# A mixer step between expert tiles: one of four late steps cut into pieces that follow expert tiles, tile loops written out as straight code

## What is computed

```python
xn = _layernorm(x)
# mixer, 256 inner channels, per sequence
x_proj, z = split(xn @ W_in.T)
x_conv = silu(causal_conv(x_proj, conv_w, 4 taps) + conv_b)
Bm, Cm, dt_in = split(x_conv @ W_x.T)
dt = softplus(dt_in @ W_dt.T + b_dt)
alpha = sigmoid(0.1 * dt)
gated = (1 - alpha) * sigmoid(mean(Bm)) * x_conv
h = scan(h = clip(alpha, 0.01, 0.99) * h + gated)      # along the sequence
y = (h * sigmoid(mean(Cm)) + D * x_conv) * silu(z)
mixer = y @ W_out.T
# experts, 8 with 256 hidden, top 2 of 8
h = silu(xt @ w1[e]) * (xt @ w3[e]);  y[e] = h @ w2[e]
moe = sum over the two chosen experts of probs * y[e]
out = x + mixer + moe
```

## Time and profile before

| | us |
|---|---|
| median of 3 runs | 474.4 (473.97 to 475.49) |
| span of the profiled execution | 553.9 |
| stage one, to the first `up` | 0 to 247.5 |
| stage two, to the end of `down(34)` | 247.5 to 483.0 |
| tail | 483.0 to 553.9 |

### The profile page before, as it was taken

The page is one execution under the profiler, slowest core; times in us unless marked ns, Lnnn a source line. Parts: engine busy times, 40 slices in busy tenths (PEclk is TensorE's granted clock), DMA queues, the critical chain, the costliest instruction groups (busy, mean ns, idle before and its releaser), DMA issues.

```text
span 553.9 us, 8718 instructions
## 1 busy us (share of the span) xinstructions
PE 459.8 (83%) x2440; PEld 324.4 (59%) x2440; DVE 394.6 (71%) x836; ACT 288.3 (52%) x406; POOL 312.4 (56%) x344
## 2 busy tenths in 40 slices
PE   0987646999999999879979869696987798979876
PEld 0884222445544455448867658585876688745455
DVE  5997551989999999878856675454635465549987
ACT  3772126878888888785533333232423232466880
POOL 4657763767767675711666656565665655663300
PEclk9999777899999999999989999797989898899999
DMA  9921114112121212235556544453543453209992
GB/s 249 283 84 52 54 64 163 50 36 83 49 77 44 82 44 72 78 98 152 164 172 179 168 134 143 120 147 122 156 135 113 126 162 107 71 2 189 243 210 80
DMA packets 48076, 65.91 MB, mean 119 GB/s; under 512 B 8424, under 2 KB 30223, under 8 KB 48048
## 3 DMA queue, kind: packets, MB, share of 16 engines
q1 hardware_dynamic: 36240, 39.56, 25.5%
q0 software_dynamic: 10656, 24.47, 16.1%
q10 hardware_dynamic: 1152, 1.57, 0.9%
HBM read 42.09 MB, written 33.83 MB: 137 GB/s over the span
## 4 chain that ended last, share of the span: by engine, by line
PE 31%; DVE 22%; another core or an unknown queue 18%; issue 16%; ACT 8%; SPq 2%; DMA 1%; DVEq 1%; ACTq 0%
PE PC L746 5%; PE PB L731 4%; PE PD L899 4%; DVE hbuf L1404 3%; PE PA L759 2%; DVE hbuf L1415 2%; DVE gbuf L1289 2%; PE PA L865 2%; PE PA L861 1%; DVE gbuf L1386 1%; DVE xnT L1690 1%; PE PA L862 1%; DVE y L1424 1%; DVE al L1389 1%
## 5 line engine op out<-in xcount | busy, mean ns | idle before, releaser
L614 POOL DMA_INDIRECT moe_out<-xnT,dst_u x142 | 143.1, 1008 | 114.7 <-DVE xnT L1690 51.2
L600 POOL DMA_INDIRECT moe_in<-xn,slot_u x128 | 137.7, 1076 | 65.6 <-issue 41.1
L1202 ACT ACTIVATE xn<-PA 128x1024 f32<-128x1024 f32 (+1 forms) x36 | 36.5, 1015 | 95.1 <-PE PA L865 52.0
L1629 DVE TENSOR_TENSOR xn<-xn,PB 128x1024 f32<-128x1024 f32 (+1 forms) x36 | 43.3, 1204 | 43.1 <-remote 19.0
L899 PE MATMUL PD<-xnT,xn 128*128 128x128 f32 x536 | 68.1, 281 | 6.1 <-DVE xnT L1690 5.7
L899 PEld LDWEIGHTS PD<-xnT,xn 128*128 128x128 f32 x536 | 64.2, 196 | 8.5 <-issue 4.9
L746 PE MATMUL PC<-xc,Wc 128*128 128x512 f32 x128 | 59.9, 612 | 2.8 <-ACT xc L1099 2.8
L759 PE MATMUL PA<-xnT,Wtap 128*128 (+4 forms) x128 | 59.1, 604 | 0.4 <-issue 0.4
L1690 DVE TENSOR_TENSOR xnT<-PD,slot_p 128x512 f32<-128x512 f32 (+1 forms) x36 | 24.5, 681 | 39.6 <-remote 35.1
L861 PE MATMUL PA<-xhi,whi 128*128 128x512 f32 x62 | 29.4, 474 | 26.6 <-ACT xhi L1196 16.7
L1196 ACT ACTIVATE xhi<-PD 128x512 fp32r<-128x512 f32 (+1 forms) x36 | 21.2, 589 | 49.7 <-remote 32.6
(11 more groups left out here) (244 smaller groups left out, 963.2 us busy)
## 6 DMA issues: line engine op xcount, KB each, us to landing
xnT<-moe_w SPq DMA_DIRECT2D x36, 256.0 KB
xn<-moe_in SPq DMA_DIRECT2D x31, 266.0 KB
out_dram<-moe_out POOLq DMA_DIRECT2D x12, 512.0 KB, 11.8
xnT<-moe_w SPq DMA_DIRECT2D x36, 128.0 KB
out_dram<-xacc SPq DMA_DIRECT2D x7, 512.0 KB, 10.0
moe_out<-xnT,dst_u POOLq DMA_INDIRECT x142
moe_in<-zrow SPq DMA_DIRECT2D x8, 266.0 KB
moe_w<-in_L_ffn_w_dram SPq DMA_DIRECT2D x2, 1024.0 KB
```

Of the source, the lines that this page charges most:

```text
L600: gp.indirect_dma_start(xs_dram, bass.IndirectOffsetOnAxis(ap=slot_u[:, k, j:j + 1], axis=0), xn_row[:, j, :], None).then_inc(s_scat, 16)
L614: gp.indirect_dma_start(yt_dram, bass.IndirectOffsetOnAxis(ap=dst_u[:, t, j:j + 1], axis=0), yo[t % OUTS][:, j, :], None, bounds_check=PAI ...
L1202: act.activation(halves(sil, t), halves(PA[:, :], t), ACT.Silu).then_inc(s_sil, 1)
L1629: ve.tensor_tensor(halves(hid[b], t), halves(sil, t), halves(PB[:, :], t), ALU.mult).then_inc(s_hid, 1)
```

## The change

With `INNER_STEPS = 1` all of step 12 runs in stage two, cut into twelve pieces. Piece n follows the tile in `INNER_AT` on every engine (tiles 1, 3, 6, 8, 11, 14, 17, 19, 21, 24, 27 and 30). The first five pieces of step 13 (`STEPS_B = 13`) follow tiles 31 to 35. So that PA, PB and PD stay with the experts, all of it goes through PC: ScalarE copies the gates out of PC to `held_g` (`hold_among`), and `gates`, `out`, `project`, `convolved` and `gated` get twins that write PC, a few matmuls each.

On TensorE the pieces are `spread`, `gates`, `out` and the two halves of `project` (pieces 1 to 5), two halves of `convolved` (8, 9) and `gated` (10). On ScalarE piece 6 is a table load, Exp, Ln and a table load back. On VectorE the pieces are the chain in eight parts, `turn`, `add_out`, `softplus` and three taps. The tail then starts at step 13 behind its `project`. The loops over tiles on TensorE, ScalarE and VectorE become straight code; the one on SyncE stays, with one 512 KB store (`store_base`, before ahead of its loop) now behind it. SyncE starts the first weight loads one mixer step earlier (it waits for 11, not 12).

```diff
+INNER_STEPS = 1
+STEPS_B = STEPS_A + INNER_STEPS
+CYCLE = 30 // INNER_STEPS
+INNER_AT = (1, 3, 6, 8, 11, 14, 17, 19, 21, 24, 27, 30)
@@ sync @@
-            sp.wait_ge(s_xp, 12)
-            sp.wait_ge(s_z, 12)
+            sp.wait_ge(s_xp, 11)
+            sp.wait_ge(s_z, 11)
...
-            store_base(STORED - 2)
             with sp.Fori(0, (FULL - 4) // 2) as i:
...
+            store_base(STORED - 2)
@@ tensor @@
+            def project_among(g, c_):
+                slot = g % SLOT3
+                if c_ == 1:
+                    pe.wait_ge(s_lt, g + 1)
+                else:
+                    pe.wait_ge(s_add, g)
+                for k in range(HALVES):
+                    last = pe.matmul(PC[:, c_ * GROUP:(c_ + 1) * GROUP], Wc[:, k, c_ * P:(c_ + 1) * P],
+                                     xc[:, slot, k, :], start=(k == 0), stop=(k == 1))
+                if c_ == 0:
+                    last.then_inc(s_u, 1)
...
+            def mixer_piece(g, at):
+                if at == 1:
+                    spread(g)
+                elif at == 2:
+                    gates_among(g)
+                elif at == 3:
+                    out(g, g % SLOT3, True)
+                elif at == 4:
+                    project_among(g, 1)
+                elif at == 5:
+                    project_among(g, 0)
+                elif at == 8 and g < STEPS_B:
+                    convolved_among(g, 0)
+                elif at == 9 and g < STEPS_B:
+                    convolved_among(g, 1)
+                elif at == 10 and g < STEPS_B:
+                    gated_among(g)
...
-            with pe.Fori(0, (FULL - 4) // 2) as i:
...
-            for t in range(2 + (FULL - 4) // 2 * 2, MOE_TILES):
+            for t in range(2, MOE_TILES):
...
                 down(t - 1, (t - 1) // 2, (t - 1) % 2, False)
-            project(STEPS_A, STEPS_A % SLOT3, True)
+                for piece in pieces(t):
+                    mixer_piece(*piece)
...
-            gates(STEPS_A, STEPS_A % SLOT3, True)
-            for g in range(STEPS_A, GROUPS - 1):
+            for g in range(STEPS_B, GROUPS - 1):
@@ scalar @@
+            def mixer_piece(g, at):
+                if at == 1:
+                    hold_among(g)
+                    decay_th(g)
+                elif at == 2:
+                    decay_al(g)
+                elif at == 4:
+                    row_tanh(g)
+                elif at == 5:
+                    abs_among(g)
+                elif at == 6 and g < STEPS_B:
+                    act.preload_act_table_set("natural_log_exp_and_others")
+                    logs_among(g)
+                    act.preload_act_table_set("silu_and_others")
...
-            with act.Fori(0, turns) as i:
...
+                for piece in pieces(t):
+                    mixer_piece(*piece)
...
-            for g in range(STEPS_A, GROUPS):
+            for g in range(STEPS_B, GROUPS):
@@ vector @@
+                if at == 3:
+                    chain_among(g, 0)
+                    turn(g)
+                elif at == 4:
+                    add_out(g)
+                    chain_among(g, 1)
...
+                elif at == 7:
+                    softplus(g)
...
+                elif at == 9:
+                    for j in range(1, TAPS):
+                        tap(g, j)
...
-            turn(STEPS_A)
-            softplus(STEPS_A)
-            for g in range(STEPS_A, GROUPS - 1):
+            g = STEPS_B
+            chain_among(g, 3)
+            chain_among(g, 4)
+            softplus(g)
+            for n in (5, 6, 7):
+                chain_among(g, n)
+            for g in range(STEPS_B, GROUPS - 1):
```

More of the change, by code:

```diff
@@ L360, in is_mixed, with among_tiles, holds, pieces @@
             return isinstance(t, int) and FULL <= t < HALF
+        def among_tiles(g):
+            return isinstance(g, int) and STEPS_A <= g <= STEPS_B
         def gate_rows(g):
-            return PC if isinstance(g, int) and g == STEPS_A else PD
+            return PC if among_tiles(g) else PD
+        def holds(g):
+            return g - STEPS_A + 2
         def gated_y(c):
-            if not isinstance(c, int) or c < STEPS_A:
+            if not isinstance(c, int) or c <= STEPS_B:
                 return y2
-            return (held_g, y2, y3)[(c - STEPS_A) % 3]
+            return (y2, held_g, y3)[(c - STEPS_B) % 3]
+        def pieces(t):
+            found = [(STEPS_A + n, at + 1) for n in range(INNER_STEPS) for at in range(len(INNER_AT))
+                     if n * CYCLE + INNER_AT[at] == t]
+            last = t - INNER_STEPS * CYCLE
+            return found + [(STEPS_B, last)] if last >= 1 else found
         @block.sync
@@ L832, in _, with gates_among @@
             pe.sem_inc(s_out, 1)
-            mixer(pe, mix, 0, STEPS_A)
+            mixer(pe, mix, 0, STEPS_A - 1)
+            mixer(pe, mix, STEPS_A - 1, STEPS_A)
+            def gates_among(g):
+                slot = g % SLOT3
+                pe.wait_ge(s_xc, g + 1)
+                pe.wait_ge(s_hold, holds(g))
+                for k in range(HALVES):
+                    for j in range(STRIPS):
+                        last = pe.matmul(PC[j * STRIP:(j + 1) * STRIP, GROUP:GROUP + P], WgS[:, k, :],
+                                         xc[:, slot, k, j * P:(j + 1) * P], start=(k == 0), stop=(k == 1))
+                last.then_inc(s_g, 1)
@@ new lines, in convolved_among @@
+            def convolved_among(g, part):
+                both = PC[:, 0:GROUP].rearrange("p (s l) -> p s l", s=SPG)
+                src = source(g).rearrange("p (s l) -> p s l", s=SPG)
+                if part == 0:
+                    pe.wait_ge(s_dt, g + 1)
+                    pe.matmul(PC[:, GROUP:2 * GROUP], WinT[:, P:2 * P], source(g), start=True, stop=True).then_inc(s_xr, 1)
+                for j in range(2 * part, 2 * part + 2):
+                    last = pe.matmul(both[:, :, j:SEQ], Wtap[:, TAPS - 1 - j, :], src[:, :, 0:SEQ - j],
+                                     start=(j == 0), stop=(j == TAPS - 1))
+                if part == 1:
+                    last.then_inc(s_xp, 1)
@@ L954, in _ @@
             g = GROUPS - 1
-            pe.wait_ge(s_add, g - 1)
-            gated(g - 1)
+            if g > STEPS_B:
+                pe.wait_ge(s_add, g - 1)
+                gated(g - 1)
+            else:
+                pe.wait_ge(s_yc, MOE_TILES)
             spread(g + 1)
-            out(g, g % SLOT3, True)
+            if g > STEPS_B:
+                out(g, g % SLOT3, True)
             pe.wait_ge(s_add, g)
@@ L1212, in tile_step, with hold_among, abs_among @@
                     round_x(t + 1, 1 - b)
+            def hold_among(g):
+                act.wait_ge(s_gb, g)
+                act.wait_ge(s_ch, (g - 2) * CHAIN + C_USED)
+                act.activation(held_g[:, :, :], PC[:, :].rearrange("p (n l) -> p n l", n=2), ACT.Copy).then_inc(s_hold, 1)
+            def abs_among(g):
+                act.wait_ge(s_u, g + 1)
+                act.wait_ge(s_th, g)
+                for c_ in range(HALVES):
+                    last = act.activation(ebuf[:, c_, :], PC[:, c_ * GROUP:(c_ + 1) * GROUP], ACT.Abs,
+                                          bias=bdt[:, c_:c_ + 1])
+                last.then_inc(s_abs, 1)
@@ L1231, in _ @@
             round_x(2, 0)
+            for piece in pieces(1):
+                mixer_piece(*piece)
             round_w(3, 1, 1, False)
```

173 lines of the change are left out of this document (97 added, 76 removed).

## The result

The changed kernel takes 483.44 us (median of 4 runs, 483.01 to 483.90), the kernel before 474.37 (4 runs, 473.97 to 475.49). The ratio is 1.0203, with a 95% interval of 1.0181 to 1.0225: 9 us, or 2%, slower. The forecast was 480.5, slower.

The account below looks back on a forecast made before the run. It took TensorE, with almost no idle time, to bound stage two and a ring of waits the tail: 474.4 + 17.3 (stage two) - 11.0 (tail) = 480.7, rounded to 480.5 us; range 467.5 to 488, its own case 477 to 485.

Parts of the forecast that it names:

- Stage two of a timed run, 179 us: Stage two before: 235.5 us in the trace less 56 us of waits on an unknown releaser, 5.1 us a tile.
- The step on which the forecast rested: TensorE in stage two of a timed run: close to nothing left, 0.1 us a tile, 5 us in all.
- Stage two +17.3: Stage two: 17.3 us of moved TensorE work, less 2 hidden, plus 2 of new waits, gives +17.3 us.
- the 2 forecast: Stage two, new waits: 2 us, bounds 0 and 6, from ScalarE's piece 6 at tile 14 making later work late.
- the 2 us taken off as hidden: Stage two: moved TensorE work hidden in idle time and short waits for `xlo`, 2 us, bounds 0 and 21.
- Tail by compute −12.6: Tail, compute engines: `down(34)` to the taps for step 14 shrinks from 24.5 to 11.9 us, 12.6 us shorter.
- The DMA side: Tail: DMA sums before end 13 us ahead of the program; after, about equal to compute; 1.6 us off, leaving −11.0.
- The stores: End of the tail: the last stores come while the sums still run, 3 to 4 us of stores behind the sums.
- The loops: Tile loops: removal costed at nothing, since the branch is already hidden under the matmuls.
- The table load: ScalarE's piece 6 at tile 14: 1.28 us per table load as in the trace, without the skill's drain of about 1.38.
- 560.2 if the holes stay: Whole kernel against its profiled time, with the unknown-releaser waits unchanged: 553.9 + 17.3 - 11.0 = 560.2 us.
- TensorE has room after all: Rival, stage two: 14 of 17.3 us hide in TensorE's idle time, giving 469 us; chance 0.20.

Follow-up runs that it names:

- straight: Kernel before with its tile loops on TensorE, ScalarE and VectorE written out and no piece moved; 473.78 us against 473.83, ratio 0.9995.
- room: Kernel before with written-out tile loops plus one unused fp32 matmul behind each of tiles 13 to 26; 479.63 us, ratio 1.0110.
- after: The changed kernel itself, as profiled on a quiet chip (span 481.4 us); timed 483.44 us against 474.37 for the kernel before, ratio 1.0203.
- straight_nosums: Kernel before with written-out tile loops, without 12 of 14 accumulating DMAs and GpSimd's end waits for the sums; 467.96 us, ratio to before 0.9863.
- after_nosums_warm: Changed kernel without 12 of 14 accumulating DMAs, with 25 unused matmuls in two TensorE waits of the tail; 548.28 us, ratio 0.9768, stalling chip.

## Why the prediction was right, and where its steps were not

**Stage two of a timed run, 179 us: right, by luck in part.** Straight shows 179.8. The prediction took 56 us out, in proportion to a chain share of 29.9%, and left a part of the holes in. On a quiet chip there are none at all, and 21 of the 55.7 us that go are no holes, but matmuls that take 178.5 us instead of 199.6. The step on which the forecast rested, that TensorE has no room, holds on quiet chips; room shows it, with 12.1 us more in stage two for 14 matmuls costed at 11.9.

**Stage two +17.3: too small by 3.1 us.** It is +20.4. TensorE's busy time grew by 196.6 - 178.5 = 18.1, against the 17.3 summed up from the earlier trace rows, and its gaps from 1.3 to 3.7, 2.4 against the 2 forecast. The term that failed is the 2 us taken off as hidden. There was next to nothing to hide in, 1.3 us of idle time in the whole stage. Of the new gaps 1.1 us belong to piece 6, the term for them, and 1.5 are the waits of tile 3, behind the copy `hold_among`, which the prediction had as hidden. It had the copy's length (2.4 us with `decay_th`) and not its wait for VectorE.

**Tail by compute −12.6: too large by 1.9, of which 0.4 came back later.** Behind `down(34)` the taps for step 14 start after 22.5 us in straight and 11.8 in after: −10.7. The part of after (11.9) was right. That of before was read as 27.2 less one hole of 2.66, and 2 us of the rest were still holes. From the taps to the last add it is 43.3 and 42.9 us. The half clock of `project(14)`, which was not foreseen, costs 1.1 us in its round, and the half clock that straight has in the window from 452 makes up for it.

**The DMA side: the step that was wrong.** It said that before ends 13 us behind its DMA traffic, and that the change makes the two about equal. In straight the DMA side ends the span, 8.8 us behind the last add, and leaving the sums out gains 5.8. Two terms were wrong.

The first is the row of scatters. The step took the last scatter at 10.9 us behind `down(34)` from a trace in which TensorE's tiles take 6.5 us on average. GpSimd needs 5.15 a tile and more. In that trace it keeps up, in a timed run (4.98) it does not, and ends 12.6 us later against `down(34)`; some 6 of these are 5.15 against 4.98 over the stage, and the scatters that last longer make up the rest (an estimate: 141 x 0.06, over 8 us in all). The holes were taken out of TensorE's row and left in GpSimd's. The tile's row did not warn: it has GpSimd busy for 3.54 of 4.97 us, since the 0.30 us between two scatters count as idle. In after, stage two is long enough for GpSimd to catch up.

The second is the end itself. The sum had 3 to 4 us of stores behind the sums, and nothing for GpSimd. Measured, the stores land 2.5 us behind the last sum in after, and the drain ends the program 6.15 us behind it.

So the DMA side gains 74.6 - 62.9 = 11.7 in the tail and the compute side 11.2 (last add 65.8 and 54.6 behind `down(34)`). Two near numbers hid the error: the forecast's −11.0 stands beside −11.7. That is luck.

**Sum.** By the spans of straight and after: −0.7 ahead of stage two, +20.4, −11.7: +8.0; the medians give 9.1. The −0.7 is scatter, since the first `up` starts between 218.1 and 219.6 in the traces of quiet chips. The forecast was +6.3, and the 3 us between are those of stage two.

**The stores**, foreseen as made late by the change, take 4.4 us to landing for 128 KB, but they take 4.7 in straight too, and they do not end the program. **The loops** at nothing: 0.9995. The Trainium skill's rule that a taken branch out of the fetched window stalls for a fetch (Runtime: NRT & Kernel Launch, Instruction fetch mechanics) shows no cost here; whether these loops' branches leave that window no run shows. **The table load**, taken at its row: the two tiles around piece 6 cost 1.6 us more in all, a little under the 2 taken. With the drain that the Trainium skill (ScalarE: Activation LUTs, What ACT_TABLE_LOAD costs) adds to a switch of sets they would have cost over 4 (an estimate, 1.6 + 2 x 1.38); the measurement decides for the row.

**"560.2 if the holes stay": wrong, and with the other sign.** On chips with holes the changed kernel takes 544 where before takes 552. The rival "TensorE has room after all" put 14 of 17.3 us hidden and a ratio of 469/474.4 = 0.989. It is wrong for the chips on which the result was timed. On the others the number is right, 16 of 20 hidden and a ratio of 0.988, and the mechanism in part: about 6 of the 16 us go into idle time, as it said, and the rest into matmuls that run longer before than after. (Its turning point, 9 us hidden, is 8.3 by its own terms, 17.3 + 2 - 11.) The prediction treated the holes as something the profiler adds. Timed runs of 552 to 561 us on some chips show times as long as that trace's. What makes these chips stall stays open; nothing in a trace of one core names the releaser.

No version beat both kernels on a quiet chip. The runs point to GpSimd's row and the sums there, since straight_nosums ends 5.8 us earlier. The drain is a place to look as well: it starts behind GpSimd's own waits for the sums, and in straight_nosums, where it did not wait for them first, it ended 2.35 us behind the landing of the last sum instead of 5.9. Leaving out only those waits, with all sums kept, was not tried, nor was scattering without a bounds check.

## What to carry to other kernels

Before a trace is used for a forecast, its span has to be that of the timed runs. If it is longer, each engine's row of work has to be laid against the shorter time by itself: a queue that keeps up in the long trace (5.4 us in 6.5) can be the bound in the short one (4.98). What ends the program is to be read from the last instruction of each engine: here it was a drain that no view of busy time shows. A stage in which an engine is busy for 178.5 of 179.8 us hides nothing, and added work that costs only half of itself may have been given back behind that stage, by a queue that caught up: look at the windows, not at the total. And a change that moves work into another engine's waits can be worth −1% on one chip and +2% on another.

## What the runs showed of the hardware

Chips that run the same program differ by 16 to 18% (474 against 552 to 561 us), with waits for an unknown releaser at 10 to 17% of the chain, and a mean granted clock of 0.93 to 0.96 instead of 0.98 to 0.99 in the runs of before. An indirect scatter of 128 rows mostly takes GpSimd 0.98 us and 0.30 to the next, but 1.04 and 0.30 on average over the 142 of straight, since some last up to 2.0; a memset of 0.56 us between two of them adds only 0.41. Accumulating DMAs run at 208 to 213 GB/s with the DMA engines at a share of 1.05 to 1.07, and the 14 of them take 41.6 us from the first issue to the last packet in straight and 41.7 in after. GpSimd's closing drain, begun behind its waits for the sums, takes 5.63 us in each of the eleven traces that have all the sums. TensorE is granted half the clock from 428 us on, behind a wait of 2.3 us (and is back at 1.00 in the window from 440). A short row of unused matmuls in such waits kept it at 1.00 in after_nosums_warm up to 536 us, and it fell behind a later wait.
